# Two cross-attention blocks: the start of each attention phase is issued and shared out differently

## The reference

```python
# layer 0, attention: q from layernorm(x), k and v from ctx_1024
scores = jnp.einsum('bhqd,bhkd->bhqk', q, k) / jnp.sqrt(jnp.asarray(DH, q.dtype))
scores = scores + relative_bias              # (1, 16, 512, 512)
scores = jnp.where(key_padding_mask[:, None, None, :], scores, -jnp.inf)
attn = jax.nn.softmax(scores, axis=-1)
out = jnp.einsum('bhqk,bhkd->bhqd', attn, v)
# layer 1, attention: the same with one mask for all heads
logits = logits + mask[None, None, :, :] * -1000000000.0
# the model
x = x + jnp.tanh(g_xattn[0]) * L0_attention(layernorm(x), ctx)
x = x + jnp.tanh(g_ffn[0]) * L0_ffn(layernorm(x))
x = x + jnp.tanh(g_xattn[1]) * L1_attention(layernorm(x), ctx)
x = x + jnp.tanh(g_ffn[1]) * L1_mixture(layernorm(x))
```

## Time and profile before

| | |
|---|---|
| median of three runs | 1013.73 us (1010.68 to 1014.83) |
| profiled execution | 1013.72 us, span 1011.6 us |
| mean granted TensorE clock | 0.971 |
| busy: TensorE, VectorE, ScalarE, GpSimd | 944.7, 578.4, 482.1, 582.9 us |
| layer 0: projection, attention | to 58, 58.8 to 285.9 us |
| layer 1: projection, attention | 396.7 to 447, 447.6 to 675.8 us |

### The profile page before, as it was taken

One profiled execution on the slowest core, in us unless ns is written; L12 is line 12 of the kernel. 1 busy time (PEld: TensorE's weight loads), 2 busy tenths in 40 slices (PEclk: granted clock), 3 DMA queues, 4 the chain that ended last, 5 costly groups with the idle time before them and its releaser, 6 DMA issues. The chain is left out here.

```text
span 1011.6 us, 21397 instructions
## 1 busy us (share of the span) xinstructions
PE 944.7 (93%) x7715; PEld 537.0 (53%) x7716; DVE 578.4 (57%) x1698; ACT 482.1 (48%) x661; POOL 582.9 (58%) x620
## 2 busy tenths in 40 slices
PE   6989999999996997988999999998899999999994
PEld 3654444444464553644444444456456577777753
DVE  4867888888743123876888888837443222222226
ACT  2437777877843111326778788753301122222210
POOL 3468999999933900368999999961036222222210
PEclk9978999999997998998999999999999999999998
DMA  9581837364002160465243434111912212222143
GB/s 302 193 230 37 231 65 222 73 193 94 9 23 84 42 218 10 120 158 133 53 110 64 116 65 116 33 49 39 339 47 90 70 53 63 63 63 63 53 158 112
DMA packets 87988, 107.56 MB, mean 106 GB/s; under 512 B 10528, under 2 KB 70520, under 8 KB 87896
## 3 DMA queue, kind: packets, MB, share of 16 engines
q1 hardware_dynamic: 77192, 85.08, 30.4%
q0 software_dynamic: 4848, 14.70, 4.3%
q10 hardware_dynamic: 5856, 6.56, 2.1%
HBM read 76.92 MB, written 29.38 MB: 105 GB/s over the span
## 5 line engine op out<-in xcount | busy, mean ns | idle before, releaser
L616 ACT ACTIVATE pT<-ps 128x1024 f32<-128x1024 f32 x256 | 248.4, 1022 | 97.8 <-PE ps L488 97.5
L658 POOL TENSOR_TENSOR xT<-nmax,xT 128x512 f32<-128x512 f32 x192 | 195.5, 1040 | 20.6 <-DVE nmax L556 20.3
L658 POOL TENSOR_TENSOR s<-nmax,s 128x512 f32<-128x512 f32 x192 | 196.4, 1040 | 16.6 <-DVE nmax L556 12.4
L556 DVE CUSTOM_DVE_ANT_0 s<-ps,bias 128x512 f32<-128x512 f32 x256 | 166.1, 689 | 45.0 <-PE ps L475 43.8
L556 DVE CUSTOM_DVE_ANT_0 xT<-ps,bias 128x512 f32<-128x512 f32 x256 | 166.5, 689 | 41.6 <-PE ps L475 32.8
L475 PE MATMUL ps<-ks,qs 97*128 97x512 bf16 (+1 forms) x512 | 162.4, 397 | 10.7 <-DMA ks<-qk_scratch 4.5
L503 PE MATMUL ps<-pT,vq 128*32 128x512 f32 x1024 | 136.0, 608 | 2.4
L1186 POOL DMA_INDIRECT slots_out<-y,id x39 | 38.2, 980 | 128.6 <-DVE y L1513 128.6
L475 PEld LDWEIGHTS ps<-ks,qs 97*128 97x128 bf16 (+1 forms) x512 | 30.7, 98 | 130.3 <-DVE nmax L556 64.0
L1265 PE MATMUL ps<-gu,xgT 128*128 x312 | 98.8, 460 | 0.7 <-ACT xgT L1349 0.7
L488 PEld LDWEIGHTS ps<-ident,xT 64*128 64x128 f32 x2048 | 71.5, 143 | 29.2 <-issue 28.5
(11 more groups left out here) (173 smaller groups left out, 1179.5 us busy)
## 6 DMA issues: line engine op xcount, KB each, us to landing
bias<-in_bias SPq DMA_DIRECT2D x16, 1024.0 KB, 5.8
qk_scratch<-parts SPq DMA_DIRECT2D x64, 128.0 KB
qs<-qk_scratch SPq DMA_DIRECT2D x32, 192.0 KB, 3.4
ks<-qk_scratch SPq DMA_DIRECT2D x32, 192.0 KB, 4.0
gu<-in_gate_up SPq DMA_DIRECT2D x8, 704.0 KB, 9.7
slots_in<-zeros POOLq DMA_DIRECT2D x4, 1280.0 KB, 7.1
xg<-slots_in SPq DMA_DIRECT2D x39, 130.0 KB, 2.1
qk_scratch<-parts ACTq DMA_DIRECT2D x32, 128.0 KB
```

The costliest lines, as they stand in the source:

```text
L556: nc.vector.tensor_tensor_reduce(at.s[m % 4][:, qt, :], sb.ps[:, ring_bank(tile_place[u - 1 + hg * 64]), :], at.bias[:, j if per_head_bias ...
L616: nc.scalar.activation(at.pT[:, slot(m // HG, m % HG), 2 * half:2 * half + 2, :], sb.ps[:, 2 + 2 * half:4 + 2 * half, :], ACT.Exp).then_in ...
L658: nc.gpsimd.tensor_tensor(s, at.nmax[:, m % 4, qt:qt + 1].to_broadcast([P, S]), s, ALU.subtract).then_inc(pool_less_max, 1)
```

## The change

1. SyncE no longer waits for all stores before the load of batch 1 in the first head group, but for the two stores that it reads (`next_stored`: k's piece 2 and q's piece 9). The wait on all of them stands behind this load.
2. In layer 0 ScalarE issues the biases of heads 2 and 3 in the projection, behind its last store, in place of SyncE.
3. For m = 0 and 1 ScalarE takes two tiles and GpSimd two (`act_tiles`); TensorE's waits in `turn` count accordingly. ScalarE's wait on all stores stands behind its tiles of m = 0, and its tiles of m = 1 come behind that wait, before the first exponentials.
4. SyncE issues the zeroing, in each head group behind the load of batch 2: a quarter of the zeros, and a quarter of the numbers. GpSimd makes the row of zeros and the numbers at the start of layer 1's projection.

```diff
@@ -135,9 +135,10 @@
     proj_done, head_done = sem(tag + "proj_done"), sem(tag + "head_done")
     rest_done, mid_done, low_done = sem(tag + "rest_done"), sem(tag + "mid_done"), sem(tag + "low_done")
     stored = [sem(tag + f"stored{i}") for i in range(PARTS)]
+    NK = DC * B
     at.stored = stored
+    at.next_stored = [(stored[DC], 48), (stored[(NK + 1) % PARTS], 48 * ((NK + 1) // PARTS + 1))]
     v_done, v_copied = sem(tag + "v_done"), sem(tag + "v_copied")
-    NK = DC * B
     NT = 2 * NK
     NV = TT // 2
 
@@ -184,6 +185,9 @@
                 nc.gpsimd.memset(at.qs[KS:KS + 1, :, :, :], 1.0).then_inc(consts, 1)
                 pool.wait_ge(consts, 3)
             else:
+                nc.gpsimd.memset(sb.zeros[:, :], 0.0).then_inc(at.zeros_ready, 1)
+                nc.gpsimd.iota(sb.spare[:, :, :], pattern=[[P, SLOT_TILES], [0, DW - D]], base=2 * N,
+                               channel_multiplier=1).then_inc(at.zeros_ready, 1)
                 pool.nop().then_inc(consts, 3)
 
             nc.gpsimd.memset(at.vq[:, :, :, :, :], 0.0).then_inc(consts, 1)
@@ -300,6 +304,9 @@
             keep_x(3)
             for n in range(NK + 2, NT):
                 head(n)
+                if layer == 0 and n == NT - 1:
+                    for j in range(2, HG):
+                        load_bias(act, at, a["bias"], 0, j)
             nc.scalar.activation(sb.warm[:, 1:2], sb.ident[:, 0:1], ACT.Exp)
 
         @block.vector
@@ -408,7 +415,6 @@
     sums_ready = sem(tag + "sums_ready")
     out_done = sem(tag + "out_done")
     granted = sem(tag + "granted")
-    zeros_ready = sem(tag + "zeros_ready")
     GROUPS = H // HG
     M = HG * B
 
@@ -431,6 +437,14 @@
     tile_place = [i for i, (read, _) in enumerate(ring) if read is biased]
     out_place = [i for i, (read, _) in enumerate(ring) if read is out_done]
 
+    def act_tiles(n):
+
+        return 2 if n < 2 else 1
+
+    def less_by_act(n):
+
+        return sum(act_tiles(i) for i in range(n + 1))
+
     def ring_bank(place):
 
         return (0, 1, 7)[place % 3]
@@ -442,15 +456,26 @@
     with nc.Block() as block:
         @block.sync
         def _(sp):
+            def zero_slots(hg):
+
+                sp.wait_ge(at.zeros_ready, 2)
+                rows = slice(hg * SLOT_TILES // GROUPS, (hg + 1) * SLOT_TILES // GROUPS)
+                dst = dram.xs.rearrange("(r p) d -> p r d", p=P)[:, rows, :]
+                sp.dma_start(dst[:, :, 0:D], sb.zeros[:, :].unsqueeze(1).to_broadcast([P, SLOT_TILES // GROUPS, D])
+                             ).then_inc(zeroed, 16)
+                sp.dma_start(dst[:, :, D:DW], sb.spare[:, rows, :].bitcast(F32)).then_inc(zeroed, 16)
+
             def body(hg, first, last):
 
-                for j in range(2, HG) if first and per_head_bias else ():
-                    load_bias(sp, at, bias_dram, 0, j)
-                for i in range(PARTS) if first else ():
-                    sp.wait_ge(at.stored[i], STORED)
+                for parts_stored, count in at.next_stored if first else ():
+                    sp.wait_ge(parts_stored, count)
                 for b in range(1, B):
                     sp.wait_ge(scores_done, (hg * 4 + b) * 16 + 16)
                     load_qk(sp, at, dram, per_head_bias, hg, b)
+                    for i in range(PARTS) if first and b == 1 else ():
+                        sp.wait_ge(at.stored[i], STORED)
+                    if zeroed is not None and b == 2:
+                        zero_slots(hg)
                 if not last:
                     sp.wait_ge(scores_done, (hg * 4 + 4) * 16 + 16)
                     load_qk(sp, at, dram, per_head_bias, hg + 1, 0)
@@ -477,8 +502,8 @@
 
             def turn(hg, m):
 
-                pe.wait_ge(less_max, hg * M + m + 1)
-                pe.wait_ge(pool_less_max, 3 * (hg * M + m + 1))
+                pe.wait_ge(less_max, less_by_act(hg * M + m))
+                pe.wait_ge(pool_less_max, QT * (hg * M + m + 1) - less_by_act(hg * M + m))
                 for kt in range(QT):
                     if kt % 2 == 0:
                         pe.wait_ge(exp1 if kt else exp0, hg * M + m + 1)
@@ -600,8 +625,6 @@
             act.nop().then_inc(exp0, 1)
             act.nop().then_inc(exp1, 1)
             act.nop().then_inc(out_kept, 1)
-            for i in range(PARTS):
-                act.wait_ge(at.stored[i], STORED)
 
             def subtract_max(hg, m, qts):
 
@@ -621,14 +644,17 @@
                 act.wait_ge(out_turned, hg * B + b + 1)
                 nc.scalar.activation(at.oT[:, :], sb.ps[:, 6, :], ACT.Copy).then_inc(out_kept, 1)
 
-            subtract_max(0, 0, (0,))
-            subtract_max(0, 1, (0,))
+            subtract_max(0, 0, range(act_tiles(0)))
+            for i in range(PARTS):
+                act.wait_ge(at.stored[i], STORED)
 
             def body(hg, first, last):
                 for m in range(M):
                     b, j = m // HG, m % HG
                     if j == 3 and not (first and b == 0):
                         keep_out(*before(hg, b))
+                    if first and m == 0:
+                        subtract_max(0, 1, range(act_tiles(1)))
                     exps(hg, m, 0, exp0)
                     exps(hg, m, 1, exp1)
                     if not (last and m + 2 >= M):
@@ -642,13 +668,6 @@
             pool.nop().then_inc(turned, 8)
             pool.nop().then_inc(av_done, 2)
             pool.nop().then_inc(out_turned, 1)
-            if zeroed is not None:
-                nc.gpsimd.memset(sb.zeros[:, :], 0.0).then_inc(zeros_ready, 1)
-                nc.gpsimd.iota(sb.spare[:, :, :], pattern=[[P, SLOT_TILES], [0, DW - D]], base=2 * N,
-                               channel_multiplier=1).then_inc(zeros_ready, 1)
-                pool.wait_ge(zeros_ready, 2)
-                pool.dma_start(dram.xs.rearrange("(r p) d -> p r d", p=P)[:, :, D:DW],
-                               sb.spare[:, :, :].bitcast(F32)).then_inc(zeroed, 16)
 
             def subtract_max(hg, m, qts):
 
@@ -665,15 +684,10 @@
                     at.vq[:, b % 2, :, :, 0:DH],
                     src[:, bass.ds(hg, 1), :, :].rearrange("p g t (j d) -> p (g t) j d", j=HG)).then_inc(v_ready, 1)
 
-            subtract_max(0, 0, (1, 2, 3))
-            subtract_max(0, 1, (1, 2, 3))
+            for m in range(2):
+                subtract_max(0, m, range(act_tiles(m), QT))
 
             def body(hg, first, last):
-                if zeroed is not None:
-
-                    pool.dma_start(dram.xs.rearrange("(g r p) d -> g p r d", g=GROUPS, p=P)[
-                        bass.ds(hg, 1), :, :, 0:D].rearrange("g p r d -> (g p) r d"),
-                        sb.zeros[:, :].unsqueeze(1).to_broadcast([P, SLOT_TILES // GROUPS, D])).then_inc(zeroed, 16)
                 for m in range(M):
                     if m % HG == 1:
                         keep_values(hg, m // HG)
@@ -1158,7 +1172,7 @@
             nc.gpsimd.iota(sb.tok[:, :, D].bitcast(I32), pattern=[[P, TT]], base=0,
                            channel_multiplier=1).then_inc(rows_named, 1)
             pool.wait_ge(rows_named, 2)
-            pool.wait_ge(zeroed, 16 * (H // HG + 1))
+            pool.wait_ge(zeroed, 16 * 2 * (H // HG))
             pool.wait_ge(slots_ready, 1)
             for c in range(2):
                 if c == 1:
@@ -1621,6 +1635,7 @@
         for layer in range(2):
             at.qk_loaded = [sem(f"qk_loaded{i}") for i in range(2)]
             at.bias_loaded = [sem(f"bias_loaded{j}") for j in range(HG)]
+            at.zeros_ready = sem("zeros_ready")
             dr = Names()
             dr.qk, dr.keymask, dr.xs = scratch.qk[layer], scratch.keymask, scratch.xs
             projection_phase(nc, sem, sb, aw, at, a, dr, layer, ld, f"p{layer}_")
```

## The result

The changed kernel takes 1006.99 us (median of 11 runs, 1003.02 to 1009.77), the one before 1013.29 us in the same comparison (11 runs, 1010.68 to 1017.17). The two medians are 6.3 us apart. The ratio, which is that of the means, is 0.993, 95% interval 0.9912 to 0.9948: 7.1 us less, where 7.7 were forecast. The profiled execution has 1004.76 us, span 1002.6 us, mean clock 0.972.

The account below looks back on a forecast made before the run. TensorE bounds the middle of attention phases, unchanged; the two phase starts are stretched by late transfers and half clock. Gains of 2.5 us (layer 0) and 5.2 us (layer 1) make 7.7: 1013.7 to 1006.0 us, range 1002 to 1010.5.

Parts of the forecast that it names:

- Layer 1: Start of layer 1's attention, first scores to m = 4's transposes: gain 5.2 us, between 2.5 and 5.6 by the clock.
- The load of batch 1: SyncE's q and k load in layer 1: issued 4 us earlier, takes 5.7 us, lands before TensorE asks for it.
- the 4.49 us: TensorE's standstill before the scores of m = 4 in layer 1, waiting for batch 1's load; all of it goes.
- The tile edit: First tiles in layer 1: ScalarE takes two of four and GpSimd's issue is gone, so m = 0 starts 1.0 us earlier.
- Layer 0: Start of layer 0's attention, up to m = 4's transposes: gain 2.5 us, taken among 1.0, 2.1 and 4.3 by the clock.
- the pair of ends for SyncE's queue beside the biases: SyncE's DMA rate in layer 0 while ScalarE's queue moves biases: 188 GB/s at best, 112 GB/s with stores 3.5 us late.
- nothing is late: Layer 0, if SyncE's queue keeps 188 GB/s: biases land by about 64 us and both VectorE waits go.
- the issue from ScalarE as free: Layer 0: 1 us of bias issue and the table load end by 55 us; ScalarE has nothing until 60.
- rival B: Layer 0 gains nothing, from biases slowing the other queue or a low clock; layer 1 gives 2.5 to 5.2: 1008.5-1011; chance 0.22.
- Rival E: Layer 0: both queues together bring only 188 GB/s, SyncE's 94, 7.2 us lost; slower kernel, 1016 to 1018.5; chance 0.04.
- SyncE's zeros: Zeroing quarters behind batch 2's load in each head group: 3.5 to 14.1 us each, costing nothing, at most 1 us.
- The clock: Both attention starts: clock fell to 0.50 while TensorE stood idle between first scores; its return weighs on the gains.

Follow-up runs that it names:

- e4: Kernel before with one edit alone: ScalarE issues biases 2 and 3 in layer 0's projection; ratio to before 1.0035 (1.0007-1.0063).
- e1: Changed kernel with SyncE issuing biases 2 and 3 at the start of layer 0's attention again; ratio to before 0.9947.
- e2: Changed kernel with ScalarE issuing biases 2 and 3 at the start of the attention block, behind the barrier; ratio to before 0.9968.
- e3: Changed kernel with ScalarE issuing bias 2 behind its last projection store and bias 3 behind the barrier; ratio to before 0.9953.
- e9: The changed kernel itself, run again with nothing altered; ratio to before 0.9952 (0.9935-0.997).
- e10: Changed kernel with ScalarE issuing biases 2 and 3 in the middle of layer 0's projection; ratio to before 0.9941.
- e8: Changed kernel with the tile edit undone: ScalarE one tile, GpSimd three for m = 0 and 1 too; ratio to before 0.9958.
- e5: Kernel before with the zeroing edit alone: SyncE issues it behind batch 2's load, memset and index fill moved; ratio to before 0.9956.
- e7: Kernel before with the early load alone: batch 1's load waits only for the stores it reads; ratio to before 0.9972.
- e6: Changed kernel with the zeroing back on GpSimd, 16-byte pieces at the start of layer 1's attention; ratio to before 0.9946.
- e12: Changed kernel with each of the first eight scores of layer 1's attention repeated twice into an unread bank; 1005.09 us, ratio to before 0.9912.

## Why the prediction was right

**Layer 1, right, by its own steps.** Forecast from the first scores: m = 0 at 5.6, m = 1 at 9.4, m = 2 at 12.6, m = 3 at 15.6, m = 4 at 19.0. Measured: 5.55, 9.33, 12.13, 14.94, 18.30. VectorE and TensorE's own order are the bound, as said, and the clock came back at m = 1. The term of the sum was 5.2 and is 6.3 in this pair. Over all profiles it is the same: layer 1 with the code of before has sums of 25.79 and 27.80 (e4), and with the code of the changed kernel 19.50, 19.51, 20.84, 20.88, 21.10 and 20.83 (e1, e2, e3, e9, e10), which makes 6.4 us between the means. So this term was 1.2 us too small. The load of batch 1 was priced at 5.7 us and took 3.1 to 4.5. m = 3 was held to GpSimd's three tiles a group, 3.0 us; the groups come in 2.8, which is four tiles of VectorE and one short wait, and in e8, with three tiles from the first group on, just the same: GpSimd is not the bound there.

**Which part brings it.** The prediction took the early load as the cure of the 4.49 us. It is one of two, and either is enough: e5 (no pieces beside the load) and e7 (load ahead of the pieces) both remove it, and e6, which has the load ahead and the pieces back, does not bring it back. The tile edit, counted with GpSimd's issue as 1.0 us, only takes away what the issue of L650 had cost; the edit of the zeroing does that alone (m = 0 at 5.55 us in e5). The times alone do not rank the edits: of the runs with a part of the change only e4, the bias edit alone, has an interval that overlaps none of the others.

**Layer 0, the number right by luck and the step wrong.** The forecast was 2.5 us, and the pair of profiles shows 24.95 - 22.44 = 2.5. But the same layer's sum with the code of before is 24.95 and, in e5, 22.56; with the changed code it is 22.44, 22.63, 22.01 and 23.06 (e6, e9, e12). The means are 23.8 of two against 22.5 of four: about 1 us, within the spread of the first. (The early load alone, e7, has 22.17, and the change without the tile edit, e8, 22.15.) So this term was about 1.3 us too large and that of layer 1 1.2 us too small, and the sum of 7.7 came out near by that.

The step that failed is the pair of ends for SyncE's queue beside the biases, 188 and 112 GB/s, and with it "nothing is late" and the issue from ScalarE as free. Beside the biases the queue has 65 GB/s. The rows did not bear the two ends as they were read. The 188 GB/s at 54 to 56 us was moved by both queues, 0.20 MB by SyncE's and 0.18 by ScalarE's; that SyncE's alone has the same rate, from 56 to 60 us, is a coincidence. The 354 at 62 to 64 us was moved by SyncE's queue alone, with the biases on it, so it did not show room for a second queue beside 188. And 112 was not this queue's lowest rate beside another one: from 452 to 456 us it had 22, beside the pieces. What I priced was when the stores land (66.9 at the worst; SyncE's wait for them ends at about 66.4, which is 67.2 on the clock of the kernel before). What I did not price is that SyncE cannot hand over its last stores: 2.2 us an issue, a barrier 2.7 us late. It was made up for by a clock that came back at m = 1, where half clock to 72 us or longer was reckoned with, and by waits that no longer existed. That the biases slow the other queue and the edit gives nothing, which is rival B's first condition, is what e1 and e4 say of this edit: 0.9947 without it and 1.0035 with it alone. The groups at half clock were set at 3.7 us, while the earlier trace rows has 4.0 (64.36 to 68.38 and 73.28 to 77.28), and 75.8 + 5.3 is 81.1, not 81.5; neither slip moves the term of 2.5 beyond its spread. Rival E had the queue at 94 GB/s, which is nearer to what was measured than my end was; its cause was wrong, though, since both queues together moved 369 GB/s at 56 to 60 us.

**The rule on issuing engines.** The Trainium skill, DMA: Bandwidth & Descriptors, "Issuing engines are not separate DMA queues", says that transfers interleave on the same 16 DMA engines whichever engine starts them, and that a second issuing engine saves only the time of starting them. The traces agree in the main: SyncE's queue alone moved 354 GB/s with the biases on it, and the two together 369. Five placements of the two biases, on two queues, gave sums of 22.0 to 26.6 us in layer 0, and none took away the gap and the waits together.

**SyncE's zeros, right.** The quarters of the pieces take 0.7 to 1.1 us to issue and land in 8.0 to 8.8 us, within the bounds of 3.5 and 14.1. The two phases take 202.65 and 202.95 us from m = 4 on, against 202.6 and 202.9 before.

**The clock.** That it fell while TensorE stood idle between its first scores was right for layer 1: it fell in twelve profiles and held in the two in which the gaps were filled, so there the gaps bring it down. In layer 0 of the changed kernel it fell earlier, during the wait at the barrier: the granted clock is 0.94 from 58 to 60 us and 0.50 from 60 to 62. Why it comes back at m = 1 in one execution and at m = 4 in another stays open; no run here steers that.

## What to carry to other kernels

A transfer moved to another engine's queue does not use idle DMA time alone: look at what the first queue still has to hand over, above all ahead of a barrier, and price the issue of its last stores. Where two edits each cure the same wait, undoing one shows nothing; each has to be run alone. And a difference of 2 us in one pair of profiles is no term of a sum until the untouched code has been seen twice.

## What was not expected of the hardware

Two queues do not share the engines evenly. Beside the biases (rows of 2 KB) SyncE's queue (rows of 1 KB) had 266 of 882 packets and 0.26 MB of 1.48 MB in 4 us, 18% of the bytes, and the issue of one store of 128 KB on it went from 0.56 to 2.0 or 2.2 us. Small pieces hold the engines out of proportion: 0.05 MB in pieces of 16 bytes took 52% of them for 4 us. And at half clock a busy TensorE does not come back at once: in e7 it worked from 450.29 to 462.28 with hardly a gap at 0.50.
